# A four-layer GRU stack with an FFN behind it on one core: scan factors from PSUM to SBUF, two gate banks in place of three, five ring banks in place of four

## The chip, the cores and the metric

The kernel runs on one core of a Trainium2 chip. The metric is the device time in microseconds (us) of one execution. The core has a tensor engine (PE, its weight loads are shown as PEld), a vector engine (DVE), a scalar engine (ACT), GpSimd (POOL) and SyncE (SP), which only issues DMAs here. Each runs its own instruction list in order. They meet through semaphores alone. The on-chip memory is SBUF, and PSUM with eight banks of 128 x 512 fp32, into which PE writes.

## The reference

```python
x = x + xcond(layernorm(x), ctx, cond, fusion_W, fusion_b, gamma, beta)
x = x + ffn(layernorm(x), W_fc, ln_w, ln_b, W_proj)

# xcond, forward and backward in time with the same weights, 4 layers:
z = sigmoid(h @ Wz + bz);  h_tilde = tanh(h @ Wz + bz)     # one product serves both
a = clip(1 - z, 1e-8, 1 - 1e-8)
h_t = a_t * h_{t-1} + z_t * h_tilde_t                        # scan over 512 tokens
h = layernorm(h_new + h) * gamma + beta                      # the + h from layer 1 on
# then concat(forward, backward) @ fusion_W.T + fusion_b

# ffn: gelu(x @ sign_quantised(W_fc).T), layernorm over 2048, @ sign_quantised(W_proj).T
```

Shapes: x is 8 x 512 x 512 (batch, tokens, features), all fp32. The stack has 4 layers of 512 x 512.

## The kernel before

**Stage 1, the GRU stack.** The work is cut in 56 jobs (batch, direction, layer). In layer 0 one job serves both directions. A job has four parts m of 128 features each. Part m of job k has the number i = 4k + m. Its way through the engines is:

- PE, `mm` (L499): 12 matmuls (high and low halves of operands and weights) into a gate bank.
- ACT, `gates` (L796, L797): sigmoid of the bank into `zb`, then tanh of the same bank into `hb`. Both have three buffers in SBUF.
- DVE, `keep` (L1067): the factor max(1 - zb, tiny), written over the gate bank in PSUM. `tiny` is a PSUM column.
- POOL, `value` (L1521): hb = zb * hb.
- DVE, `scan` (L1080, in layer 0 L1088 and L1089 for the two directions): a `tensor_tensor_scan` of the factor and `hb`, 512 long, into `zb` (layer 0: into `H`).
- POOL, `add` (L1530): H = H + zb, in layers 1 to 3.

What follows a job is its tail. PE transposes H to token order (`tokens`, L519) into a ring bank, DVE takes the statistics (`stats`, L1100 to L1108), POOL the inverse root (`inv`, L1540 to L1545), ACT normalises into a buffer `ntok` (`norm`, L808), PE transposes back (`back`, L533) into a ring bank, ACT writes H and the high half AH (`feature`, L833, L837) and DVE the low half AL (`low`, L1117). AH and AL feed the next layer's matmuls.

Every engine walks over the same slots s, one job for each, with an order of operations written out by hand. The lists `RING_SLOT`, `FEAT_SLOT`, `LOW_SLOT` repeat that order, so that the semaphores' targets can be counted. Beside the jobs run preparations of the second stage's weights. In slots 24 to 55 that is on POOL `excess` (L1596 and L1598).

Of PSUM, banks 0 to 2 are the gate banks, banks 3 to 6 the ring, and bank 7 holds small things. `mm` number i waits until scan i - 3 is done, since that scan reads the factor out of its bank. A user n of the ring waits in `claim` until the last reader of user n - 4 is done.

**Stage 2** is the fusion matmul, the second layernorm and the FFN. DVE sums the activations there with L1297 and makes low halves with L1283. POOL sums the squares with L1640. These two engines' instructions have all tensors in SBUF.

Of the kernel before, what the change touches and what calls it, by code (L numbers as in the profile page):

```python
# [85 lines left out]
def batch(s):  # L86
# [129 lines left out]
def pixart_block(nc, x, wt, cond, fwt, fb, gamma, beta, fct, lnw, lnb, pjt, out):  # L216
# [64 lines left out]
    ntok = [sb(p1, f"ntok{i}", [128, 4, 512]) for i in range(3)]  # L281
# [58 lines left out]
    GATE, RING = PS[0:3], PS[3:7]  # L340
    TURNED, HIDDEN, PROJ = PS[0], (PS[1], PS[7]), PS[3:7]

    FUSED = {(u, h): RING[BANK[("F", u, h)] % 4] if u < 4 else PS[2] for u in range(NU) for h in range(2)}
# [70 lines left out]
    def _(e):  # L414
        def claim(n):

            if n < 4:
                return
            u = USERS[n - 4]
# [17 lines left out]
        def shift(l):  # L437

            n = BANK[("W", l)]
            claim(n)  # L440
            p = slice(0, 1) if l in BY_ROW else slice(0, 128)
            if l in BY_ROW:
                e.wait_ge(s_rc, BY_ROW.index(l) + 1)
            else:
                e.wait_ge(s_fo, KC * FOLDED.index(l) + KC)
            for m in range(KC):
                r = e.matmul(RING[n % 4][:, m:m + 1], bw[l][p, m * 128:(m + 1) * 128], ones[p, :], start=True, stop=True)
            r.then_inc(s_bp, 1)

        def fold_row(l):  # L450
# [16 lines left out]
        def add_rows(h):
# [5 lines left out]
            for q in range(KC):  # L473
                r = e.matmul(RING[n % 4][0:2, :], gb[:, q, :], xbuf1[:, q, :], start=(q == 0), stop=(q == KC - 1))
            r.then_inc(s_gp, 1)

        def mm(k, m):
# [5 lines left out]
            if i >= 3:  # L483
                e.wait_ge(s_sc, i - 2)
            n = 0
            for q in range(KC):
# [11 lines left out]
                for w, a in ((WH[l], AH[s]), (WL[l], AH[s]), (WH[l], AL[s])):  # L498
                    r = e.matmul(GATE[i % 3][:], w[:, q, m * 128:(m + 1) * 128], a[:, q, :], start=(n == 0), stop=(n == 11))  # L499
# [3 lines left out]
        def tokens(tau, pr):  # L503
# [11 lines left out]
            for i in range(2):  # L515
                n, c = BANK[("T", tau, pr, i)], (2 * pr + i) * 128
                claim(n)
                for m in range(KC):
                    r = e.transpose(RING[n % 4][:, m * 128:(m + 1) * 128], H[s][:, m, c:c + 128], ident[:])  # L519
                r.then_inc(s_t1, 1)  # L520

        def back(what, idx, m):
# [3 lines left out]
            n, w = BANK[(what, idx, m)], NTOK[(what, idx)] % 3  # L526
# [5 lines left out]
            for i in range(4):  # L532
                r = e.transpose(RING[n % 4][:, i * 128:(i + 1) * 128], ntok[w][:, i, m * 128:(m + 1) * 128], ident[:])  # L533
# [35 lines left out]
        def fc(j):  # L569
# [5 lines left out]
            if j == 0:  # L575
                e.wait_ge(d_fc, 32)
# [131 lines left out]
        for s in SLOTS:  # L708
            if s == SUM_SLOT:
                add_up()  # L710
            if s in ROW_SLOT:
                add_rows(ROW_SLOT.index(s))
            mm(job(s), 0)
            back("x", batch(s + 1), 1)
            back("x", batch(s + 1), 0)
            back("h", tail_b(s - 3), 2)
            back("h", tail_b(s - 3), 1)
            mm(job(s), 1)
            back("h", tail_b(s - 3), 3)
# [9 lines left out]
            mm(job(s), 3)  # L729
            tokens(tail_b(s - 2), 1)  # L730
            tokens(tail_b(s - 1), 0)
# [40 lines left out]
    def _(e):  # L772
# [7 lines left out]
        def gates(k, m):  # L780
# [15 lines left out]
            e.activation(zb[c][:], GATE[c][:], ACT.Sigmoid, bias=bias[:, l, m:m + 1]).then_inc(s_z, 1)  # L796
            e.activation(hb[c][:], GATE[c][:], ACT.Tanh, bias=bias[:, l, m:m + 1]).then_inc(s_t, 1)  # L797

        def norm(tau, pr):
# [5 lines left out]
            if w >= 3 and NORMED[p] < NORMED[("h", tau, 1 - pr)]:  # L805
                e.wait_ge(s_t2, max(T2N[(*NTOK_OF[w - 3], m)] for m in range(KC)) + 1)
            for i in range(2):
                e.activation(ntok[w % 3][:, 2 * pr + i, :], RING[BANK[("T", tau, pr, i)] % 4][:], ACT.Identity,  # L808
                             bias=nbp[:, r, i:i + 1], scale=rsp[:, r, i:i + 1]).then_inc(s_nt, 1)

        def norm_x(b):
# [5 lines left out]
            if w >= 3:  # L817
                e.wait_ge(s_t2, max(T2N[(*NTOK_OF[w - 3], m)] for m in range(KC)) + 1)
            for i in range(4):
                if b == 0 and i % 2 == 0:  # L820
                    e.wait_ge(s_xb, i // 2 + 1)
                e.activation(ntok[w % 3][:, i, :], (xbuf1 if b == 1 else xbuf)[:, i, :], ACT.Identity, bias=nb[:, b % 2, i:i + 1],
                             scale=rs[:, b % 2, i:i + 1]).then_inc(s_xn, 1)

        def feature(what, idx, m):
# [4 lines left out]
            n, s = BANK[u] % 4, 2 * (idx % 2) if what == "x" else place(TAILS[idx])  # L830
# [23 lines left out]
        def take_row(l):  # L854

            e.wait_ge(s_fr, BY_ROW.index(l) + 1)
            e.activation(bw[l][0:1, :], RING[BANK[("V", l)] % 4][0:1, :], ACT.Copy).then_inc(s_rc, 1)

        def take_rows(h):
# [5 lines left out]
            e.activation(dst, RING[BANK[("G", h)] % 4][0:2, :], ACT.Copy).then_inc(s_gr, 1)  # L865
# [8 lines left out]
        def aside(s):  # L874
# [3 lines left out]
            if PREP0 + 8 < s <= PREP0 + NPREP:  # L878
                sign(s - PREP0 - 1)
            if ABS0 <= s < ABS0 + 16:  # L880
                absolute(2 * (s - ABS0))
                absolute(2 * (s - ABS0) + 1)
# [125 lines left out]
        for s in SLOTS:  # L1008
            feature("h", tail(s - 4), 0)
            feature("h", tail(s - 4), 1)  # L1010
            feature("h", tail_b(s - 5), 0)
            feature("h", tail(s - 4), 3)
            feature("x", batch(s - 1), 3)
# [46 lines left out]
    def _(e):  # L1060
        def keep(k, m):
# [5 lines left out]
            e.scalar_tensor_tensor(GATE[c][:], zb[c][:], 1.0, tinyp.broadcast_to([128, S]), ALU.subtract, ALU.max,  # L1067
                                   reverse0=True).then_inc(s_a, 1)

        def scan(k, m):  # L1070
# [17 lines left out]
            e.tensor_tensor_scan(H[s][:, m, :], GATE[c][:], hb[c][:], 0.0, ALU.mult, ALU.add).then_inc(s_sf, 1)  # L1088
            e.tensor_tensor_scan(H[s + 1][:, m, :][:, ::-1], GATE[c][:, ::-1], hb[c][:, ::-1], 0.0, ALU.mult,  # L1089
                                 ALU.add).then_inc(s_sc, 1)  # L1090

        def stats(tau, pr):
# [17 lines left out]
        def low(what, idx, m):  # L1110
# [6 lines left out]
            e.tensor_tensor(AL[s][:, m, :], RING[BANK[u] % 4][:], AH[s][:, m, :].bitcast(F32), ALU.subtract).then_inc(s_al, 1)  # L1117
# [62 lines left out]
        def biases(l):  # L1180

            e.wait_ge(s_bp, l)
            e.tensor_tensor(cnd[:, l, :], RING[BANK[("W", l)] % 4][:, 0:KC], condt[:, l, :], ALU.add).then_inc(s_cn, 1)

        def aside(s):
# [3 lines left out]
            if s == ABS0 + 16:  # L1189
                for w in range(2):  # L1190
                    e.wait_ge(s_abs, 32)
                    e.reduce_sum(ssum[:, w:w + 1], asum[:, 16 * w:16 * w + 16], axis=AX_X).then_inc(s_ss, 1)
# [786 lines left out]
```

## Time and profile before

| | |
|---|---|
| median of 3 runs | 1590.77 us (1590.26 to 1591.34) |
| span of the profiled execution | 1589.6 us |
| its own time beside the span | none is given; the median lies 1.2 us above the span |
| PE busy in the span | 1532.7 us, 96% |
| DVE | 1372.7 us, 86% |
| POOL | 1127.2 us, 71% |
| ACT | 1030.8 us, 65% |
| granted TensorE clock | 1.00 of full speed in all slices |

Busy time is the time in which an engine executes something. Waits on semaphores are not in it. A wait for anything inside an instruction is in it and makes that instruction longer.

### The profile page before, as it was taken

What the parts mean: (1) busy time and instruction counts of PE and PEld (TensorE: products, weight loads), DVE (VectorE), ACT (ScalarE), POOL (GpSimd) and SP (SyncE); (2) the same over time, 40 slices, a digit from 0 to 9 for tenths busy, and PEclk for the clock granted to TensorE, in tenths of its full rate; (3) what the DMA queues carried; (4) which work ended last, traced back from release to release, by engine and by line L of the source; (5) the groups of instructions that cost most, each with busy time, mean ns of one, the idle gap of its engine ahead of it and who ended that gap; (6) DMA issues with size and microseconds to landing.
All of it is one profiled execution on the core that took longest, in us unless ns stands there. A gap on an engine that the chain in (4) does not pass through costs nothing.

```text
span 1589.6 us, 22972 instructions
## 1 busy us (share of the span) xinstructions
PE 1532.7 (96%) x7690; PEld 1255.9 (79%) x7690; DVE 1372.7 (86%) x2155; ACT 1030.8 (65%) x1689; POOL 1127.2 (71%) x1028
## 2 busy tenths in 40 slices
PE   7999999989989999999999999999999999999999
PEld 5777877777878778878778878888888888888887
DVE  7987999988999989899988897888887878787877
ACT  6887878888677788677787734444444444445454
POOL 4876877778979779979779864665565656555666
PEclk9999999999999999999999999999999999999999
DMA  4111231412302010312214462020201111120101
GB/s 166 41 53 54 74 97 36 145 55 87 126 34 87 34 54 34 120 35 79 93 39 154 154 221 84 20 87 20 85 22 60 47 61 47 39 68 23 45 14 40
DMA packets 72866, 112.68 MB, mean 71 GB/s; under 512 B 5159, under 2 KB 37927, under 8 KB 69678
## 3 DMA queue, kind: packets, MB, share of 16 engines
q1 hardware_dynamic: 72750, 111.21, 20.7%
q8 instruction: 63, 1.03, 0.3%
q14 instruction: 53, 0.43, 0.1%
HBM read 73.43 MB, written 37.76 MB: 70 GB/s over the span
## 4 chain that ended last, share of the span: by engine, by line
PE 66%; POOL 12%; DVE 9%; ACT 8%; issue 4%; DMA 0%; SPq 0%; POOLq 0%; DVEq 0%; ACTq 0%
PE ps L499 17%; PE ps L585 15%; PE ps L604 14%; PE ps L553 11%; POOL hb L1521 4%; POOL H L1530 4%; PE ps L533 3%; PE ps L519 3%; DVE bnp L1100 2%; ACT ntok L808 2%; ACT hb L797 2%; DVE H L1088 2%; DVE H L1089 1%; POOL rsp L1542 1%; DVE AL L1117 1%
## 5 line engine op out<-in xcount | busy, mean ns | idle before, releaser
L499 PE MATMUL ps<-AH,WH 128*128 128x512 f32 x896 | 366.9, 410 | 6.8 <-DVE H L1089 5.0
L1521 POOL TENSOR_TENSOR hb<-zb,hb 128x512 f32<-128x512 f32 x224 | 289.3, 1292 | 111.4 <-ACT hb L797 110.8
L499 PE MATMUL ps<-AL,WH 128*128 128x512 f32 x896 | 350.8, 392 | 0.0
L499 PE MATMUL ps<-AH,WL 128*128 128x512 f32 x896 | 350.0, 391 | 0.0
L1640 POOL TENSOR_TENSOR acq<-acq,sq 128x512 f32<-128x512 f32 x120 | 181.8, 1515 | 152.0 <-ACT sq L926 151.3
L1080 DVE TENSOR_TENSOR_SCAN zb<-ps,hb 128x512 f32<-128x512 f32 x192 | 234.1, 1219 | 38.6 <-POOL hb L1521 35.4
L1530 POOL TENSOR_TENSOR H<-H,zb 128x512 f32<-128x512 f32 x192 | 249.1, 1298 | 7.5 <-DVE zb L1080 5.1
L913 ACT ACTIVATE g<-ps 128x512 f32<-128x512 f32 x128 | 76.5, 598 | 249.3 <-PE ps L585 249.3
L1283 DVE SCALAR_TENSOR_TENSOR gl<-g,wcol,gh 128x512 fp32r<-128x512 f32 x118 | 133.6, 1132 | 93.3 <-ACT gh L923 93.3
L796 ACT ACTIVATE zb<-ps,cnd 128x512 f32<-128x512 f32 x192 | 133.1, 693 | 121.2 <-PE ps L499 110.8
L499 PEld LDWEIGHTS ps<-AH,WH 128*128 128x128 f32 x896 | 168.7, 188 | 42.1 <-DVE H L1089 7.7
L499 PEld LDWEIGHTS ps<-AL,WH 128*128 128x128 f32 x896 | 168.3, 188 | 37.1
L499 PEld LDWEIGHTS ps<-AH,WL 128*128 128x128 f32 x896 | 169.1, 189 | 29.4
L1297 DVE TENSOR_TENSOR acc<-acc,g 128x512 f32<-128x512 f32 x120 | 189.3, 1577 | 0.0
L1117 DVE TENSOR_TENSOR AL<-ps,AH 128x512 fp32r<-128x512 f32 x224 | 148.8, 680 | 27.6 <-ACT AH L837 26.8
L1100 DVE BATCH_NORM_STATS2 bnp<-ps 128x6 f32<-128x512 f32 x256 | 163.6, 680 | 2.0 <-PE ps L519 1.9
L808 ACT ACTIVATE ntok<-ps,nbp,rsp 128x512 f32<-128x512 f32 x192 | 139.2, 780 | 35.7 <-POOL nbp L1545 35.4
L833 ACT ACTIVATE H<-ps,bet,gam 128x512 f32<-128x512 f32 x192 | 154.6, 805 | 10.4 <-PE ps L533 10.0
L1067 DVE SCALAR_TENSOR_TENSOR ps<-zb,ps 128x512 f32<-128x512 f32 x224 | 152.6, 681 | 8.2 <-ACT hb L797 7.8
L519 PE MATMUL ps<-ident,H 128*128 128x128 f32 x1024 | 135.1, 274 | 16.5 <-ACT ntok L808 11.5
L533 PE MATMUL ps<-ident,ntok 128*128 128x128 f32 x896 | 121.0, 278 | 27.8 <-ACT ntok L808 13.8
L533 PEld LDWEIGHTS ps<-ident,ntok 128*128 128x128 f32 x896 | 102.2, 142 | 55.6 <-ACT ntok L808 31.2
(172 smaller groups left out, 3356.2 us busy)
## 6 DMA issues: line engine op xcount, KB each, us to landing
hs_scratch<-H SPq DMA_DIRECT2D x16, 1024.0 KB, 5.5
hc<-hs_scratch SPq DMA_DIRECT2D x32, 512.0 KB, 4.4
xr<-in_x SPq DMA_DIRECT2D x32, 256.0 KB, 4.5
out<-ob SPq DMA_DIRECT2D x32, 256.0 KB, 2.2
xbuf<-in_x SPq DMA_DIRECT2D x7, 1024.0 KB, 8.6
RAW<-in_wt SPq DMA_DIRECT2D x16, 256.0 KB, 7.1
stg<-in_fct SPq DMA_DIRECT2D x16, 256.0 KB, 3.3
stg<-in_pjt SPq DMA_DIRECT2D x16, 256.0 KB, 2.7
```

Source lines behind the costliest of these rows:

```text
L499: r = e.matmul(GATE[i % 3][:], w[:, q, m * 128:(m + 1) * 128], a[:, q, :], start=(n == 0), stop=(n == 11))
L519: r = e.transpose(RING[n % 4][:, m * 128:(m + 1) * 128], H[s][:, m, c:c + 128], ident[:])
L533: r = e.transpose(RING[n % 4][:, i * 128:(i + 1) * 128], ntok[w][:, i, m * 128:(m + 1) * 128], ident[:])
L553: r = e.matmul(FUSED[u, h][:], a[u % 2][:, q, :], w[:, q, :], start=(n == 0), stop=(n == 11))
L585: r = e.matmul(HIDDEN[j % 2][:], FC[q][:, c * 128:(c + 1) * 128], a[b % 2][:, q, :], start=(n == 0), stop=(n == 7))
L604: r = e.matmul(PROJ[t][:], a[BUFFER[j]][:, t * 128:(t + 1) * 128], PJ[c], start=(c == 0 and a is gh), stop=(c == NC - 1 and a is gl))
L1080: e.tensor_tensor_scan(zb[c][:, rv], GATE[c][:, rv], hb[c][:, rv], 0.0, ALU.mult, ALU.add).then_inc(s_sc, 1)
L1100: e.bn_stats(bnp[:, r, i, :], RING[BANK[u] % 4][:]).then_inc(s_bs, 1)
L1297: e.tensor_tensor(acc[b % 2][:], acc[b % 2][:], g[j % 2][:], ALU.add).then_inc(f_s1, 1)
L1521: e.tensor_tensor(hb[c][:], zb[c][:], hb[c][:], ALU.mult).then_inc(s_p, 1)
L1530: e.tensor_tensor(H[s][:, m, :], H[s][:, m, :], zb[i % 3][:], ALU.add).then_inc(s_v, 1)
L1640: e.tensor_tensor(acq[b % 2][:], acq[b % 2][:], sq[:], ALU.add).then_inc(f_s2, 1)
```

## The change

- The factor goes to a new SBUF tile `ab` (three buffers), and the scans read both inputs from SBUF.
- With that the gate banks are free after the tanh. There are two of them (PS[0] and PS[2]), and `mm` number i waits for tanh i - 2.
- The ring has five banks, and a user n waits for user n - 5.
- `ntok` has two buffers where it had three, which makes room for `ab`. `norm` waits for the backs of the tail two before it.
- In the second stage `fc(0)` has one more wait (`f_x1` at 8), since its bank is in the ring now.
- The slot lists and the calls in the slot loops are written in another order. The reordered pairs never both exist in one slot, so each engine issues the same operations in the same order as before.

```diff
-    ntok = [sb(p1, f"ntok{i}", [128, 4, 512]) for i in range(3)]
+    ntok = [sb(p1, f"ntok{i}", [128, 4, 512]) for i in range(2)]
+    ab = [sb(p1, f"ab{i}", [128, S]) for i in range(3)]
+    sb(p1, "free", [128, 512])
...
-    GATE, RING = PS[0:3], PS[3:7]
+    GATE = (PS[0], PS[2])
+    RING = [PS[(1, 3, 4, 5, 6)[(i - BANK[("F", 3, 1)]) % 5]] for i in range(5)]
...
         def claim(n):
 
-            if n < 4:
-                return
-            u = USERS[n - 4]
+            if n < 5:
+                return
+            u = USERS[n - 5]
...
-            if i >= 3:
-                e.wait_ge(s_sc, i - 2)
+            if i >= 2:
+                e.wait_ge(s_t, i - 1)
...
-                    r = e.matmul(GATE[i % 3][:], w[:, q, m * 128:(m + 1) * 128], a[:, q, :], start=(n == 0), stop=(n == 11))
+                    r = e.matmul(GATE[i % 2][:], w[:, q, m * 128:(m + 1) * 128], a[:, q, :], start=(n == 0), stop=(n == 11))
...
             if j == 0:
+                e.wait_ge(f_x1, 8)
                 e.wait_ge(d_fc, 32)
...
-            if w >= 3 and NORMED[p] < NORMED[("h", tau, 1 - pr)]:
-                e.wait_ge(s_t2, max(T2N[(*NTOK_OF[w - 3], m)] for m in range(KC)) + 1)
+            if w >= 2 and NORMED[p] < NORMED[("h", tau, 1 - pr)]:
+                e.wait_ge(s_t2, max(T2N[(*NTOK_OF[w - 2], m)] for m in range(KC)) + 1)
...
-            e.scalar_tensor_tensor(GATE[c][:], zb[c][:], 1.0, tinyp.broadcast_to([128, S]), ALU.subtract, ALU.max,
+            e.scalar_tensor_tensor(ab[c][:], zb[c][:], 1.0, tinyp.broadcast_to([128, S]), ALU.subtract, ALU.max,
                                    reverse0=True).then_inc(s_a, 1)
...
-                e.tensor_tensor_scan(zb[c][:, rv], GATE[c][:, rv], hb[c][:, rv], 0.0, ALU.mult, ALU.add).then_inc(s_sc, 1)
+                e.tensor_tensor_scan(zb[c][:, rv], ab[c][:, rv], hb[c][:, rv], 0.0, ALU.mult, ALU.add).then_inc(s_sc, 1)
...
-            e.tensor_tensor_scan(H[s][:, m, :], GATE[c][:], hb[c][:], 0.0, ALU.mult, ALU.add).then_inc(s_sf, 1)
-            e.tensor_tensor_scan(H[s + 1][:, m, :][:, ::-1], GATE[c][:, ::-1], hb[c][:, ::-1], 0.0, ALU.mult,
+            e.tensor_tensor_scan(H[s][:, m, :], ab[c][:], hb[c][:], 0.0, ALU.mult, ALU.add).then_inc(s_sf, 1)
+            e.tensor_tensor_scan(H[s + 1][:, m, :][:, ::-1], ab[c][:, ::-1], hb[c][:, ::-1], 0.0, ALU.mult,
                                  ALU.add).then_inc(s_sc, 1)
```

## Rows read from the trace of the kernel before

**Rows 1.** Windows by stage: length, then busy time of each engine (instructions), clock, DMA share.

```profile
0.00:923.00 923.00, 869.54 (x4678) 712.18 (x4679) 828.12 (x1549) 727.05 (x1213) 739.94 (x754) 1.00 0.23 81
923.00:1589.00 666.00, 663.19 (x3013) 543.70 (x3012) 544.63 (x607) 303.74 (x477) 387.25 (x275) 1.00 0.18 57
```

**Rows 2.** Groups of PE's matmuls, 0 to 923: busy, mean ns, idle before them.

```profile
L499 PE MATMUL ps<-AH,WH 128*128 128x512 f32 x896 | 366.9, 410 | 6.8 <-DVE H L1089 5.0 <-DVE zb L1080 1.8
...
L519 PE MATMUL ps<-ident,H 128*128 128x128 f32 x1008 | 133.2, 274 | 16.5 <-ACT ntok L808 11.5 <-DVE AL L1117 5.0
L533 PE MATMUL ps<-ident,ntok 128*128 128x128 f32 x896 | 121.0, 278 | 27.8 <-ACT ntok L808 13.8 <-ACT ntok L822 10.9 <-DVE AL L1117 2.6
```

**Rows 3.** The chain of waits from 512 to 560: start, us, what.

```profile
512.98 1.31 POOL hb L1521
514.28 1.24 POOL H L1530
...
520.24 1.25 POOL hb L1521
...
529.80 1.11 DVE H L1089
```

**Rows 4.** Groups of DVE, 0 to 923.

```profile
L1080 DVE TENSOR_TENSOR_SCAN zb<-ps,hb 128x512 f32<-128x512 f32 x192 | 234.1, 1219 | 38.6 <-POOL hb L1521 35.4
...
L1067 DVE SCALAR_TENSOR_TENSOR ps<-zb,ps 128x512 f32<-128x512 f32 x224 | 152.6, 681 | 8.2 <-ACT hb L797 7.8
L1117 DVE TENSOR_TENSOR AL<-ps,AH 128x512 fp32r<-128x512 f32 x224 | 148.8, 680 | 27.6 <-ACT AH L837 26.8
L1088 DVE TENSOR_TENSOR_SCAN H<-ps,hb 128x512 f32<-128x512 f32 x32 | 39.0, 1219 | 8.9 <-POOL hb L1521 5.2 <-issue 3.2
```

**Rows 5.** Groups of POOL, 0 to 923.

```profile
L1521 POOL TENSOR_TENSOR hb<-zb,hb 128x512 f32<-128x512 f32 x224 | 289.3, 1292 | 111.4 <-ACT hb L797 110.8
L1530 POOL TENSOR_TENSOR H<-H,zb 128x512 f32<-128x512 f32 x191 | 247.9, 1298 | 7.5 <-DVE zb L1080 5.1 <-ACT H L833 2.3
...
L1598 POOL TENSOR_TENSOR stg<-raw,stg 128x512 f32<-128x512 f32 x32 | 41.3, 1292 | 2.7
```

**Rows 6.** Single lines: count, duration min/median/max in ns.

```profile
L1080 DVE TENSOR_TENSOR_SCAN zb<-ps,hb x192: 1205/1223/1226, 61.1 to 921.5; 128x512 f32<-128x512 f32 x192
...
L1297 DVE TENSOR_TENSOR acc<-acc,g x120: 676/1779/1794, 952.3 to 1576.4; 128x512 f32<-128x512 f32 x120
```

**Rows 7.** DVE's timeline in stage 2, two stretches: start, us, what.

```profile
952.30 0.68 DVE L1297 TENSOR_TENSOR acc<-acc,g 128x512 f32<-128x512 f32 x1
...
1003.42 1.77 DVE L1283 SCALAR_TENSOR_TENSOR gl<-g,wcol,gh 128x512 fp32r<-128x512 f32 x1
```

**Rows 8.** POOL's timeline from 1003.

```profile
1003.32 1.33 POOL L1640 TENSOR_TENSOR acq<-acq,sq 128x512 f32<-128x512 f32 x1 [0.37 <-ACT sq L926]
1004.61 1.73 POOL L1662 TENSOR_TENSOR x<-x,cB 128x512 f32<-128x512 f32 x1
```

**Rows 9.** DVE's timeline, 510 to 516 (stage 1).

```profile
511.19 1.22 DVE L1080 TENSOR_TENSOR_SCAN zb<-ps,hb 128x512 f32<-128x512 f32 x1 [0.18 <-POOL hb L1521]
...
512.91 1.28 DVE L1117 TENSOR_TENSOR AL<-ps,AH 128x512 fp32r<-128x512 f32 x2
514.39 1.22 DVE L1080 TENSOR_TENSOR_SCAN zb<-ps,hb 128x512 f32<-128x512 f32 x1 [0.20 <-POOL hb L1521]
```

**Rows 10.** POOL's timeline, the same stretch.

```profile
511.04 0.71 POOL L1540 TENSOR_TENSOR rl<-vep,nhalf 128x2 f32<-128x2 f32 x1
511.72 1.30 POOL L1530 TENSOR_TENSOR H<-H,zb 128x512 f32<-128x512 f32 x1
512.98 1.31 POOL L1521 TENSOR_TENSOR hb<-zb,hb 128x512 f32<-128x512 f32 x1
514.23 1.29 POOL L1530 TENSOR_TENSOR H<-H,zb 128x512 f32<-128x512 f32 x1
515.57 1.29 POOL L1521 TENSOR_TENSOR hb<-zb,hb 128x512 f32<-128x512 f32 x1
```

More of the change, by code:

```diff
@@ L339, in pixart_block @@
     PS = [ctx.enter_context(nc.psum_tensor(f"ps{i}", [128, 512], F32)) for i in range(8)]
-    GATE, RING = PS[0:3], PS[3:7]
+    GATE = (PS[0], PS[2])
+    RING = [PS[(1, 3, 4, 5, 6)[(i - BANK[("F", 3, 1)]) % 5]] for i in range(5)]
     TURNED, HIDDEN, PROJ = PS[0], (PS[1], PS[7]), PS[3:7]
-    FUSED = {(u, h): RING[BANK[("F", u, h)] % 4] if u < 4 else PS[2] for u in range(NU) for h in range(2)}
+    FUSED = {(u, h): RING[BANK[("F", u, h)] % 5] if u < 4 else PS[2] for u in range(NU) for h in range(2)}
     tinyp = PS[7][:, 0:1]
@@ L525, in back @@
                 return
-            n, w = BANK[(what, idx, m)], NTOK[(what, idx)] % 3
+            n, w = BANK[(what, idx, m)], NTOK[(what, idx)] % 2
             if what == "h":
@@ L729, in _ @@
             mm(job(s), 3)
+            tokens(tail_b(s - 1), 0)
             tokens(tail_b(s - 2), 1)
-            tokens(tail_b(s - 1), 0)
             tokens(tail(s - 1), 1)
@@ L816, in norm_x @@
                 e.wait_ge(s_xb, b + 2)
-            if w >= 3:
-                e.wait_ge(s_t2, max(T2N[(*NTOK_OF[w - 3], m)] for m in range(KC)) + 1)
+            if w >= 2:
+                e.wait_ge(s_t2, max(T2N[(*NTOK_OF[w - 2], m)] for m in range(KC)) + 1)
             for i in range(4):
@@ L821, in norm_x @@
                     e.wait_ge(s_xb, i // 2 + 1)
-                e.activation(ntok[w % 3][:, i, :], (xbuf1 if b == 1 else xbuf)[:, i, :], ACT.Identity, bias=nb[:, b % 2, i:i + 1],
+                e.activation(ntok[w % 2][:, i, :], (xbuf1 if b == 1 else xbuf)[:, i, :], ACT.Identity, bias=nb[:, b % 2, i:i + 1],
                              scale=rs[:, b % 2, i:i + 1]).then_inc(s_xn, 1)
@@ L829, in feature @@
             u = (what, idx, m)
-            n, s = BANK[u] % 4, 2 * (idx % 2) if what == "x" else place(TAILS[idx])
+            n, s = BANK[u] % 5, 2 * (idx % 2) if what == "x" else place(TAILS[idx])
             e.wait_ge(s_t2, T2N[u] + 1)
@@ L856, in take_row @@
             e.wait_ge(s_fr, BY_ROW.index(l) + 1)
-            e.activation(bw[l][0:1, :], RING[BANK[("V", l)] % 4][0:1, :], ACT.Copy).then_inc(s_rc, 1)
+            e.activation(bw[l][0:1, :], RING[BANK[("V", l)] % 5][0:1, :], ACT.Copy).then_inc(s_rc, 1)
         def take_rows(h):
@@ L864, in take_rows @@
             dst = (raw0[0:2, :], xbuf1[0:2, 0, :])[h]
-            e.activation(dst, RING[BANK[("G", h)] % 4][0:2, :], ACT.Copy).then_inc(s_gr, 1)
+            e.activation(dst, RING[BANK[("G", h)] % 5][0:2, :], ACT.Copy).then_inc(s_gr, 1)
         def sign(n):
@@ L1182, in biases, with centred, sums_abs @@
             e.wait_ge(s_bp, l)
-            e.tensor_tensor(cnd[:, l, :], RING[BANK[("W", l)] % 4][:, 0:KC], condt[:, l, :], ALU.add).then_inc(s_cn, 1)
-        def aside(s):
+            e.tensor_tensor(cnd[:, l, :], RING[BANK[("W", l)] % 5][:, 0:KC], condt[:, l, :], ALU.add).then_inc(s_cn, 1)
+        def centred(s):
             if PREP0 <= s < PREP0 + 8:
                 center(s - PREP0)
[L1189 to L1192, printed above, removed]
+        def sums_abs():
+            for w in range(2):
+                e.wait_ge(s_abs, 32)
+                e.reduce_sum(ssum[:, w:w + 1], asum[:, 16 * w:16 * w + 16], axis=AX_X).then_inc(s_ss, 1)
         def bias_rows(h):
@@ L1200, in bias_rows @@
                 e.wait_ge(s_gv, 1)
[L1201 removed]
+            e.tensor_tensor(fbb[0:2, :], RING[BANK[("G", h)] % 5][0:2, :], fbb[0:2, :], ALU.add).then_inc(s_gv, 1)
         def center(n):
```

77 lines of the change are left out of this document (41 added, 36 removed).

## The prediction

> **What bounds the kernel now.** I read the windows first, cut at the end of the stack [rows 1]. In stage 2 (923 to 1589 us) PE is busy 663 of 666 us, and the change adds only one wait there (below). So everything is decided in stage 1: 923 us, PE busy 869.5, DVE 828.1, POOL 739.9, ACT 727.1. PE is idle 53 us, DVE 95, POOL 183. The reader is to see that two engines are near their limit at once. Next come PE's groups, for what ended its idle time [rows 2]: of its waits 6.8 us are for scans, which hold a gate bank, 5.0 + 2.6 for L1117 and 11.5 for L808, which hold a ring bank. The other 13.8 and 10.9 us of L533 I count as waits for data. That is 25.9 us which more banks could give back. Last the chain of waits inside stage 1 [rows 3]: it runs over POOL's products and adds, piece behind piece, and then over DVE's scans. DVE and POOL set the pace in such slots, and PE has waits because they are late. A cost on these two is a cost in time.
>
> **The change, part by part.** *The order of operations* is what it was: the pairs that change places (an x and a tail's transposes) never both exist in a slot. 0 us.
>
> *Keep writes SBUF.* L1067 has one SBUF tensor and a PSUM column in, and now SBUF out. The nearest row is L1117, one PSUM and one SBUF tensor in, SBUF out: 680 ns against 681 [rows 4]. I take 0; the bound is their difference, 224 x 1 ns, on either side.
>
> *Two gate banks.* Mm i waits for tanh i - 2 where it waited for scan i - 3. Between the two lie a POOL product and a scan on the other side of the tanh, so the wait gets shorter: at most 6.8 us back [rows 2], at least 0. *Five ring banks*: at most 11.5 + 5.0 + 2.6 = 19.1 us back, at least 0. I take 0 for both in the sum, since a PE that starts earlier still hands its result to DVE and POOL, which are slower after the change (next part).
>
> *Two ntok buffers.* Norm's new wait is for the backs of the tail two before. On PE those backs stand ahead of the tokens whose normalisation waits, so the tokens themselves come later than what is waited for. 0; if it did wait, the gates behind it on ACT would be late, and with them keep and value. *fc(0)'s wait for x1*: feat(3) stands ahead of it on PE and needs the same x1. 0.
>
> *The scans read two SBUF tensors.* This is the part that costs. First what the trace shows of DVE and POOL side by side. The scan, whose factor is in PSUM, takes 1205 to 1226 ns in all 192 cases [rows 6], though POOL is busy in 80% of the stage [rows 1]: it is never disturbed. L1297 has both inputs in SBUF. Alone it takes 0.68 us [rows 7]; over its 120 cases it is 676 at least and 1779 in the median [rows 6]. How it comes to that shows at 1003 us [rows 7, 8]. L1283 starts at 1003.42, while POOL's L1640 runs from 1003.32 to 1004.65. It ends at 1005.19, that is 0.54 after POOL's end, where it would need 0.68 alone: it stood still until 0.14 before POOL's end. And POOL's next one, L1662, started at 1004.61, ends at 1006.34, 1.15 after L1283's end: it stood still too, until 0.14 before DVE's end, and then took its 1.29. So one waits for the other whole instruction, and they take turns. After the change each scan has this form, and POOL's products and adds have it already.
>
> The Trainium skill (SBUF — State Buffer, "Who interferes with whom") says the same and speaks against this change: a vector instruction with two SBUF inputs contends with a GpSimd instruction that reads SBUF, and the second one to start blocks until the first is through. No run here shows a scan with two SBUF inputs; by that rule the sum below stands, without it the first rival does.
>
> What it costs in a slot I step through at 511 us [rows 9, 10]. Before: scan 511.19 to 512.41; add 511.72 to 513.02; product 512.98 to 514.28; then the next scan, which waited for it, 514.39 to 515.61; the add behind it had started at 514.23, 0.05 before the product's end; product 515.57 to 516.86. After: the first scan starts beside the small 128x2 POOL operation (511.04), which I take as no hindrance. The add stands until 512.41 - 0.14 = 512.27 and ends at 513.56. The product, 1.31 long and starting 0.04 before that end as it did before, ends at 514.83. The scan is ready at 514.93, but the add started at 514.78, ends at 516.07, and holds it until 515.93: the scan ends at 517.15, 1.54 late. The next product waits for that and ends at 518.30, 1.44 late. Two scans cost 1.5 us on both engines, 0.75 each.
>
> The bounds of this price. Below: timing independent of each other. POOL's 128x512 operations with SBUF inputs are 289.3 + 247.9 + 41.3 us [rows 5], with L1596 and small groups about 636 (an estimate), 69% of 923. A scan that starts beside one waits half of 1.29 less 0.14, 0.5 us: 0.69 x 0.5 = 0.34 us a scan. Above: each scan waits for a whole one, 1.29 - 0.14 = 1.15. The two scans of a layer-0 part come back to back, with a product queued between [rows 3, 4], and pay near that. There are 192 + 32 + 32 = 256 scans (L1089 has as many as L1088). I take 0.7, by the stepped slot, the nearest row: 256 x 0.7 = 179 us on DVE; bounds 87 and 294.
>
> Not all of that becomes time. DVE's 95 us of idle are partly waits for PE and ACT (26.8 for L837, 7.8 for L797 [rows 4]), and these shrink when DVE is what is late. I let 54 us be absorbed, some 60% of the idle, which leaves DVE 828 + 179 = 1007 busy in 1048 us. POOL has as much room: 740 + about 150 of standing still.
>
> **Sum.** 1589.6 (span) + 0 (order, keep, ntok, fc) - 0 (banks) + 179 - 54 = 1714.6, and 1.2 between this execution's span and the median of the runs: 1716 us, 8% slower.
>
> **The rivals.** *The lock bites, but the idle time swallows most of it.* For it: 95 and 183 us of idle. Against it: the chain lies on POOL and DVE themselves. At 0.34 us a scan, 87 us, with half absorbed: +44, 1635; the case reaches from 1596 to 1640.
>
> *The scan isn't hindered* (other side). It needs 1.22 us for 512 elements where L1117 needs 0.68 [rows 4], so it reads at half the pace and might share with POOL. Nothing else speaks for it. Then the banks are all that is left: 25.9 us at most, half of it passed on: -13, 1578, from 1565 to 1589. It decides if a scan's added time stays under some 0.1 us: 256 x 0.1 = 26.
>
> *POOL becomes the bound outright.* In the slots with L1596 and L1598 its work is densest, the chain lies on it [rows 3], and every product waits for a scan before it can release the next. At 1.0 us a scan and no more than 54 absorbed: 256 - 54 = +202, 1793; from 1765 up.
>
> *Nothing moves*: the scan isn't hindered and PE's waits only change their name: 1591.
>
> **How the numbers follow.** Within 0.2% (3.2 us) a measurement can't tell the kernels apart. Forecast (1640 to 1765): 0.70. Absorbed: 0.12. POOL bound: 0.07. Unhindered scan: 0.08. Nothing: 0.03. Range: leaving out the fastest 0.11 and the slowest 0.07 gives 1615 to 1770. Slower 0.89, same 0.03, faster 0.08.
>
> **What would show it.** L1080's group: a mean well over 1219 ns, 1.7 to 2.1 us, minimum near 1.2, maximum near 2.4. L1521 and L1530 over 1292 ns, with maxima near 2.3. L1067's group unchanged at about 681. DVE's busy time in stage 1 near 1000 us, the stage near 1048 long, stage 2 still about 666. PE's waits for scans at its gate banks gone from the list, but its idle time larger, for L808 and L1117. I am wrong if the scans' mean stays at 1.22, or if it is 1.9 and the stage is hardly longer.

## The result, and the profile after

| | before | changed |
|---|---|---|
| median of 4 runs | 1590.97 us | 1713.28 us (1711.91 to 1714.78) |
| ratio | | 1.077, 95% interval 1.0757 to 1.0783 |
| span of the profiled execution | 1589.6 us | 1710.0 us |

The change makes the kernel 122 us slower; 1716 was forecast. The windows of the changed kernel, cut where its last scan ends, answer to [rows 1]:

```profile
0.00:1043.00 1043.00, 900.52 (x4684) 739.67 (x4685) 911.73 (x1549) 726.92 (x1213) 896.01 (x754) 0.97 0.21 72
1043.00:1710.00 667.00, 662.32 (x3008) 542.52 (x3006) 545.44 (x607) 303.10 (x476) 387.51 (x275) 1.00 0.17 57
```

Stage 1 is 120 us longer (1043 against 923), stage 2 is what it was. In stage 1 DVE is busy 84 us more, POOL 156 us more, ACT as long as before. The granted clock is 0.97: 19 times in the stage it fell to the lower of its two levels (1.2 and 2.4 GHz). PE is busy 31 us more. DVE's idle time, 95 us before, is now 131.

The groups of DVE and of POOL in stage 1 answer to [rows 4] and [rows 5]:

```profile
L1088 DVE TENSOR_TENSOR_SCAN zb<-ab,hb 128x512 f32<-128x512 f32 x192 | 301.1, 1568 | 71.3 <-POOL hb L1533 69.8
...
L1075 DVE SCALAR_TENSOR_TENSOR ab<-zb,ps 128x512 f32<-128x512 f32 x224 | 150.0, 670 | 6.6 <-ACT hb L801 6.3
L1125 DVE TENSOR_TENSOR AL<-ps,AH 128x512 fp32r<-128x512 f32 x224 | 145.9, 675 | 30.2 <-ACT AH L841 30.2
L1097 DVE TENSOR_TENSOR_SCAN H<-ab,hb 128x512 f32<-128x512 f32 x32 | 49.6, 1550 | 0.0
L1096 DVE TENSOR_TENSOR_SCAN H<-ab,hb 128x512 f32<-128x512 f32 x32 | 47.6, 1489 | 13.3 <-issue 7.8 <-POOL hb L1533 5.1
```
```profile
L1533 POOL TENSOR_TENSOR hb<-zb,hb 128x512 f32<-128x512 f32 x224 | 355.8, 1589 | 79.1 <-ACT hb L801 78.9
L1542 POOL TENSOR_TENSOR H<-H,zb 128x512 f32<-128x512 f32 x191 | 260.2, 1362 | 8.7 <-DVE zb L1088 8.7
...
L1557 POOL TENSOR_TENSOR nbp<-nmp,rsp 128x2 f32<-128x2 f32 x96 | 55.4, 577 | 14.1 <-POOL rsp L1554 0.4
L1608 POOL TENSOR_SCALAR stg<-raw,th,nth 128x512 f32<-128x512 f32 x32 | 51.7, 1614 | 0.0
L1610 POOL TENSOR_TENSOR stg<-raw,stg 128x512 f32<-128x512 f32 x32 | 41.1, 1286 | 2.7
```

Two groups of POOL before, for comparison with L1608 and L1557:

```profile
L1596 POOL TENSOR_SCALAR stg<-raw,th,nth 128x512 f32<-128x512 f32 x32 | 24.8, 775 | 0.0
...
L1545 POOL TENSOR_TENSOR nbp<-nmp,rsp 128x2 f32<-128x2 f32 x96 | 20.2, 210 | 14.1 <-POOL rsp L1542 0.4
```

The reader is to see three things. First, the scans grew from 1219 to 1568 ns in the mean, and keep, next to them and on the same new tile, did not grow (670 against 681). Second, on POOL those instructions grew that start while a scan runs. Of the products 84 of 224 do, and take 2.09 us in the mean; the other 140 take 1.29. Of L1608 (L1596 before) 30 of 32 do, and its mean went from 775 to 1614 ns. L1610, right behind it, never does, and kept its length (1286 ns against 1292). Third, DVE's wait for the product rose from 35.4 to 69.8 us.

How an instruction gets longer shows in the timelines of DVE and POOL from 540 us. They are the same kind of stretch as [rows 9, 10]:

```profile
540.33 2.03 DVE L1088 TENSOR_TENSOR_SCAN zb<-ab,hb 128x512 f32<-128x512 f32 x1
542.28 0.66 DVE L1075 SCALAR_TENSOR_TENSOR ab<-zb,ps 128x512 f32<-128x512 f32 x1
542.97 1.84 DVE L1088 TENSOR_TENSOR_SCAN zb<-ab,hb 128x512 f32<-128x512 f32 x1
```
```profile
540.01 1.26 POOL L1533 TENSOR_TENSOR hb<-zb,hb 128x512 f32<-128x512 f32 x1 [0.48 <-ACT hb L801]
542.44 1.29 POOL L1542 TENSOR_TENSOR H<-H,zb 128x512 f32<-128x512 f32 x1 [1.16 <-DVE zb L1088]
543.69 2.21 POOL L1533 TENSOR_TENSOR hb<-zb,hb 128x512 f32<-128x512 f32 x1
```

The product runs to 541.27, and the scan that started at 540.33 ends at 542.36, 1.09 later. The add runs to 543.73, and the next scan ends at 544.81, 1.08 later. The product of 543.69 starts inside that scan and ends at 545.90, 1.09 after it. The forecast of an undisturbed length less 0.14 us holds for the scan to 0.01 (1.22 - 0.14 = 1.08). For the product it would be 1.15, and it is 0.06 less.

These are no picked cases. 115 of the 256 scans take over 1.24 us, and 110 of these end 1.06 to 1.11 us after the POOL instruction beside which they started. Of the products and adds that start inside a scan, 109 take over 1.4 us, and all of them end 1.05 to 1.10 us after that scan. The 22 scans that start while POOL runs nothing are all undisturbed. This is the turn-taking that [rows 7, 8] showed for other instructions of stage 2. The rule of the Trainium skill (SBUF — State Buffer, "Who interferes with whom") that the second one to start stands still agrees, and the trace now shows it for the scan too.

PE's groups answer to [rows 2]:

```profile
L502 PE MATMUL ps<-AH,WH 128*128 128x512 f32 x896 | 375.7, 419 | 3.0 <-ACT hb L801 1.5 <-DVE AL L1125 1.4
...
L536 PE MATMUL ps<-ident,ntok 128*128 128x128 f32 x896 | 134.0, 298 | 111.4 <-ACT ntok L812 95.5 <-ACT ntok L826 11.1 <-DVE AL L1125 4.9
L522 PE MATMUL ps<-ident,H 128*128 128x128 f32 x1008 | 133.6, 275 | 27.1 <-POOL H L1542 11.4 <-ACT ntok L812 8.1 <-DVE AL L1125 6.4
```

The waits for scans at the gate banks are gone, as meant. In their place stands the wait for ACT's normalisation, 95.5 us where it was 13.8. Read by itself this row accuses `ntok`, which lost a buffer. The list of all waits leads one step further: that normalisation waited for POOL (35.4 us before, 120.7 now), and the list has no wait of it for a buffer. The row before, then the row after (us in total, times, longest):

```profile
ACT ntok L808 <- POOL nbp L1545: 35.4, 38, 2.2
```
```profile
ACT ntok L812 <- POOL nbp L1557: 120.7, 73, 3.9
```

### The profile page after: what moved, and what is told of

Its sections match the earlier page's. It is cut to its first block, busy times and chain, and to the rows that moved or that the text cites. A ratio compares the mean times of both kernels' runs of the same rounds, so it can differ in the third digit from the quotient of the medians.

```text
span 1710.0 us, 22973 instructions
## 1 busy us (share of the span) xinstructions
PE 1562.8 (91%) x7690; PEld 1282.2 (75%) x7690; DVE 1457.2 (85%) x2155; ACT 1030.0 (60%) x1689; POOL 1283.5 (75%) x1028
## 4 chain that ended last, share of the span: by engine, by line
PE 44%; POOL 29%; DVE 13%; issue 8%; ACT 5%; DMA 0%; POOLq 0%; SPq 0%; DVEq 0%; ACTq 0%
PE ps L589 14%; PE ps L608 13%; POOL hb L1533 10%; PE ps L556 10%; POOL H L1542 8%; PE ps L502 3%; POOL rsp L1554 3%; DVE zb L1088 3%; DVE bnp L1108 2%; POOL nbp L1557 2%; PE ps L536 2%; DVE AL L1125 2%; POOL stg L1608 2%; DVE H L1096 2%; POOL stg L1610 1%
## 5 line engine op out<-in xcount | busy, mean ns | idle before, releaser
L1533 POOL TENSOR_TENSOR hb<-zb,hb 128x512 f32<-128x512 f32 x224 | 355.8, 1589 | 79.1 <-ACT hb L801 78.9
L502 PE MATMUL ps<-AH,WH 128*128 128x512 f32 x896 | 375.7, 419 | 3.0 <-ACT hb L801 1.5
L1088 DVE TENSOR_TENSOR_SCAN zb<-ab,hb 128x512 f32<-128x512 f32 x192 | 301.1, 1568 | 71.3 <-POOL hb L1533 69.8
L502 PE MATMUL ps<-AH,WL 128*128 128x512 f32 x896 | 357.3, 399 | 0.0
L502 PE MATMUL ps<-AL,WH 128*128 128x512 f32 x896 | 356.4, 398 | 0.0
L1542 POOL TENSOR_TENSOR H<-H,zb 128x512 f32<-128x512 f32 x192 | 261.4, 1362 | 8.7 <-DVE zb L1088 8.7
L536 PE MATMUL ps<-ident,ntok 128*128 128x128 f32 x896 | 134.0, 298 | 111.4 <-ACT ntok L812 95.5
L536 PEld LDWEIGHTS ps<-ident,ntok 128*128 128x128 f32 x896 | 113.1, 152 | 139.1 <-ACT ntok L812 112.2
L812 ACT ACTIVATE ntok<-ps,nbp,rsp 128x512 f32<-128x512 f32 x192 | 139.1, 777 | 120.8 <-POOL nbp L1557 120.7
L502 PEld LDWEIGHTS ps<-AH,WH 128*128 128x128 f32 x896 | 174.7, 195 | 36.7 <-ACT hb L801 2.6
L1075 DVE SCALAR_TENSOR_TENSOR ab<-zb,ps 128x512 f32<-128x512 f32 x224 | 150.0, 670 | 6.6 <-ACT hb L801 6.3
```

The lines of the kernel that those rows point to most:

```text
L502: r = e.matmul(GATE[i % 2][:], w[:, q, m * 128:(m + 1) * 128], a[:, q, :], start=(n == 0), stop=(n == 11))
L536: r = e.transpose(RING[n % 5][:, i * 128:(i + 1) * 128], ntok[w][:, i, m * 128:(m + 1) * 128], ident[:])
L1088: e.tensor_tensor_scan(zb[c][:, rv], ab[c][:, rv], hb[c][:, rv], 0.0, ALU.mult, ALU.add).then_inc(s_sc, 1)
L1533: e.tensor_tensor(hb[c][:], zb[c][:], hb[c][:], ALU.mult).then_inc(s_p, 1)
L1542: e.tensor_tensor(H[s][:, m, :], H[s][:, m, :], zb[i % 3][:], ALU.add).then_inc(s_v, 1)
```

## The experiments

Kernels of one group ran on the same chip beside the kernel before (1590.9 to 1592.0 us there). Where two experiments of different groups are compared, each one's ratio is.

### Parts of the change alone, and the suspected cost taken away

**The factors alone in SBUF.** The kernel before with `ab`, and two `ntok` buffers for the room.

```diff
-    ntok = [... for i in range(3)]
+    ntok = [... for i in range(2)]
+    ab = [sb(p1, f"ab{i}", [128, S]) for i in range(3)]
...
-            e.scalar_tensor_tensor(GATE[c][:], zb[c][:], 1.0, ...
+            e.scalar_tensor_tensor(ab[c][:], zb[c][:], 1.0, ...
...
-                e.tensor_tensor_scan(zb[c][:, rv], GATE[c][:, rv], hb[c][:, rv], ...
+                e.tensor_tensor_scan(zb[c][:, rv], ab[c][:, rv], hb[c][:, rv], ...
```

> The kernel before with the factors in SBUF (and two ntok buffers, which makes the room), but with its three gate banks, released by the scan, and its four ring banks. Theory (a scan with two SBUF inputs and a POOL operation that reads SBUF exclude each other): all of the loss comes with this edit alone, 1705 to 1725 us, the scans' mean duration 1.5 to 1.6 us with a maximum near 2.25, POOL's products near 1.6 us. Rival (the shorter list of gate banks or the new waits do it): at most 1.5% above the kernel before, 1615 us. If the new banks give something back inside the change, this kernel is slower than the changed one by up to 25 us.

Measured: 1717.17 us, ratio 1.0787 (1.077 to 1.0803). The interval overlaps with that of the whole change, so the 4 us between the two medians are not shown to be a difference. The scans' mean is 1570 ns, the products' 1593. All of the loss comes with this edit (it has the two `ntok` buffers too, which the next run tests); the rival's 1615 is out.

**Two ntok buffers alone.**

```diff
-            if w >= 3 and NORMED[p] < NORMED[("h", tau, 1 - pr)]:
-                e.wait_ge(s_t2, max(T2N[(*NTOK_OF[w - 3], m)] for m in range(KC)) + 1)
+            if w >= 2 and NORMED[p] < NORMED[("h", tau, 1 - pr)]:
+                e.wait_ge(s_t2, max(T2N[(*NTOK_OF[w - 2], m)] for m in range(KC)) + 1)
```

> The kernel before with two ntok buffers in place of three and nothing else. Theory: the wait for the tail two before is always over, 1590 to 1592 us, no difference. Rival (the longer idle time of PE for the normalisation, 112 us of waits on ACT's ntok in the changed kernel, comes from the missing third buffer): 1600 us or more.

Measured: 1591.11 us, ratio 0.9999 (0.999 to 1.0008). In the kernel before the third buffer is not needed. In the changed one the normalisation is idle for POOL alone, as shown above. So PE's 95.5 us of waits for it are the trail of POOL's lateness and not of the buffer.

**The changed kernel, scans with one SBUF input.** Every bank, buffer and wait of the change stays. Each scan, the two of layer 0 included, reads a PSUM column in place of `hb` and so leaves out the GRU's second operand.

```diff
-                e.tensor_tensor_scan(zb[c][:, rv], ab[c][:, rv], hb[c][:, rv], 0.0, ALU.mult, ALU.add).then_inc(s_sc, 1)
+                e.tensor_tensor_scan(zb[c][:, rv], ab[c][:, rv], tinyp.broadcast_to([128, S]), 0.0, ALU.mult, ALU.add).then_inc(s_sc, 1)
```

> The changed kernel whole, with its banks, buffers and waits, but each scan reads a PSUM column spread over 512 as its second input in place of hb, so it has one SBUF input; the scan's result is then not the GRU's. Theory: scans back to 1.22 us each and none longer, POOL's products back to 1.29, 1575 to 1591 us: the loss is gone and what the banks give shows alone (at most 25.9 us). Rival (waits of the change, a bank less for the gates, or the clock of PE): still above 1650 us.

Measured: 1591.32 us, ratio 1.0001 (0.9992 to 1.001). Its groups of scans and of POOL's products:

```profile
L1088 DVE TENSOR_TENSOR_SCAN zb<-ab,ps 128x512 f32<-128x512 f32 x192 | 233.5, 1216 | 39.7 <-POOL hb L1533 36.7
```
```profile
L1533 POOL TENSOR_TENSOR hb<-zb,hb 128x512 f32<-128x512 f32 x224 | 288.9, 1290 | 111.7 <-ACT hb L801 111.4
```

With a PSUM column in place of the second SBUF input scans and products have their old lengths, and the 122 us are gone. The loss needs the second SBUF input; all the rest of the change together comes to 0.4 us, within the noise. The last group returns to the banks.

**A PSUM bank for the factors, two gate banks.** An attempt at the gain without the price.

```diff
-    GATE, RING = PS[0:3], PS[3:7]
+    GATE, FACT, RING = (PS[0], PS[2]), PS[1], PS[3:7]
...
-            if i >= 3:
-                e.wait_ge(s_sc, i - 2)
+            if i >= 2:
+                e.wait_ge(s_t, i - 1)
...
+            if i > 0:
+                e.wait_ge(s_sc, i)
-            e.scalar_tensor_tensor(GATE[c][:], zb[c][:], 1.0, ...
+            e.scalar_tensor_tensor(FACT[:], zb[c][:], 1.0, ...
```

> The kernel before with one PSUM bank for the factors and two gate banks released by the tanh: keep i waits for scan i - 1, which stands ahead of it on DVE in any case. Scans keep one SBUF input. Ring and ntok as before. Theory: the waits of PE's gate matmuls for scans (6.8 us) go, and 0 to 7 us come back, 1584 to 1591 us. Rival (a gate bank less costs something since tanh now holds PE): 1595 us or more.

Measured: 1600.04 us, ratio 1.0056 (1.0043 to 1.0068). I expected a small gain and got a loss of 9.1 us, in the range of the rival, though PE's waits for scans are gone from its trace too. Below it is taken apart as far as it was tested.

### How much of it, and through which engine

**Half of the scans.**

```diff
+            f = GATE[c] if m < 2 else ab[c]
-            e.scalar_tensor_tensor(GATE[c][:], zb[c][:], 1.0, ...
+            e.scalar_tensor_tensor(f[:], zb[c][:], 1.0, ...
...
-                e.tensor_tensor_scan(zb[c][:, rv], GATE[c][:, rv], hb[c][:, rv], ...
+                e.tensor_tensor_scan(zb[c][:, rv], f[:, rv], hb[c][:, rv], ...
```

> As the kernel with the factors alone in SBUF, but the parts 0 and 1 of each job keep their factor in the gate bank, so half of the 256 scans have two SBUF inputs. Theory: half of those scans can be hindered, and half of the loss of that kernel shows: 1640 to 1670 us, and no scan that reads a factor from PSUM is over 1.24 us. Rival (the loss is a threshold, an engine that tips over into being the bound): all of it, 1700 us or more, or nearly nothing, under 1605 us.

Measured: 1644.51 us, ratio 1.0344 (1.0328 to 1.036), 53 us, 0.42 us for each of the 128 scans. It is neither all nor nearly nothing, so there is no threshold of the kind that the rival had. Where the loss sits surprised me. The scans from SBUF and from PSUM in layers 1 to 3 of this kernel:

```profile
L1084 DVE TENSOR_TENSOR_SCAN zb<-ab,hb 128x512 f32<-128x512 f32 x96 | 121.3, 1264 | 18.3 <-POOL hb L1525 17.0
L1084 DVE TENSOR_TENSOR_SCAN zb<-ps,hb 128x512 f32<-128x512 f32 x96 | 117.1, 1220 | 49.6 <-POOL hb L1525 48.7
```

The 96 scans from SBUF are hardly longer (1264 ns). That has to do with the half that was chosen, parts 2 and 3. Most of their scans start beside one of POOL's 128x2 operations: 105 of 128 in this kernel and in the changed one. In the changed kernel 100 of its 115 long scans are of parts 0 and 1, and 15 of parts 2 and 3. So this run is not half of the changed kernel's disturbed scans, and the 0.42 is no price that holds for either half. But the 96 scans from PSUM, none of them over 1.226 us, wait 48.7 us for POOL's products. DVE is idle 49.6 us before them, where before the same scans it was 29.4. DVE's busy time in its stage 1 is 838.3 us, 10 us more than before, and POOL's 810.9, 71 more. A stretch of it shows how that goes:

```profile
567.47 1.22 DVE L1092 TENSOR_TENSOR_SCAN H<-ab,hb 128x512 f32<-128x512 f32 x1
568.61 1.20 DVE L1093 TENSOR_TENSOR_SCAN H<-ab,hb 128x512 f32<-128x512 f32 x1
```
```profile
567.70 0.98 POOL L1549 TENSOR_TENSOR nbp<-nmp,rsp 128x2 f32<-128x2 f32 x1
568.64 2.25 POOL L1525 TENSOR_TENSOR hb<-zb,hb 128x512 f32<-128x512 f32 x1
```

No scan is longer than 1.22. POOL's small operation of 0.20 us starts inside the first scan and takes 0.98, and the product behind it starts inside both and takes 2.25, to 1.08 after the end of the second. DVE goes first and POOL pays, and POOL's next product is what later scans wait for.

**Layer 0 alone.** `f = ab[c] if JOBS[k][2] == 0 else GATE[c]`, otherwise as the one above.

> The same with the factor in SBUF in layer-0 jobs alone: 64 scans, 32 pairs back to back on DVE, where POOL's product of the next part is queued between the two. Theory, by the price of a scan in the changed kernel (122 us over 256 scans, 0.48 us each): 64 x 0.48 = 31 us, 1622 us, 1610 to 1640. If back-to-back pairs pay 1.05 us a scan, as the prediction's upper step has it: 1658 us.

Measured: 1624.96 us, ratio 1.0212 (1.0198 to 1.0226), 34 us, 0.53 us for each of 64 scans. The prediction had such pairs pay near its upper bound, 1.15 us (the expectation above says 1.05), and they cost less than half of that.

**A busier PE.** The changed kernel with one matmul of each gate product issued twice.

```diff
+                if q == 0:
+                    e.matmul(GATE[i % 2][:], WH[l][:, q, m * 128:(m + 1) * 128], AH[s][:, q, :], start=True, stop=True)
                 for w, a in ((WH[l], AH[s]), (WL[l], AH[s]), (WH[l], AL[s])):
```

> The changed kernel with the first matmul of each gate product issued twice, 224 matmuls of 0.2 us more (45 us of PE), the result unchanged. It asks whether the short falls of the granted clock in stage 1 (3.4 us at half speed each, 20 and more of them) are part of the loss. Theory (they are not, PE is not what is late): the falls get fewer, and the time stays within 5 us of the changed kernel, 1708 to 1720. Rival (the clock costs some 30 us, the rise of PE's busy time): 1690 or less if the falls go away.

Measured: 1717.85 us, ratio 1.0798 (1.0783 to 1.0813), against 1.077 for the change. The granted clock over the whole kernel is 0.988 where it was 0.980. The falls were fewer, not gone, and the time did not get shorter; PE is busy 38 us more in stage 1 (938.4 us against 900.5), and the kernel takes some 5 us more. So PE has room there. There are 12 falls in the stage where there were 19. Since they didn't all go away, this shows for a part of them only that the lower clock costs nothing that one can see.

**Less work on POOL.** Two of its preparation operations cut to two columns, in the kernel before and in the changed one:

```diff
-            e.tensor_scalar(stg2[n % 2][:], raw[n % 2][:], th[:, w:w + 1], ...
+            e.tensor_scalar(stg2[n % 2][:, 0:2], raw[n % 2][:, 0:2], th[:, w:w + 1], ...
...
-            e.tensor_tensor(stg2[n % 2][:], raw[n % 2][:], stg2[n % 2][:], ALU.subtract)...
+            e.tensor_tensor(stg2[n % 2][:, 0:2], raw[n % 2][:, 0:2], stg2[n % 2][:, 0:2], ALU.subtract)...
```

> The kernel before with POOL's two preparation operations of slots 24 to 55 cut from 512 columns to 2, so that the second stage's weights are not the right ones. It takes some 60 us of work off POOL. All theories: a little faster than before or the same, 1575 to 1591 us, since POOL stands in the chain of these slots.

> The changed kernel with the same cut. Against the other one with the cut it shows the loss when POOL has less to do. Theory (scans and POOL take turns, POOL's queue hands the delay on): the loss falls from 122 us to 90 to 110, since 64 of about 500 POOL operations that exclude a scan are gone. Rival (POOL is the bound outright in those slots): the loss falls by half or more, to 60 us or less. Rival (POOL's work doesn't matter, DVE alone carries it): it stays at 122.

Measured: 1585.99 and 1700.82 us, 115 us apart, where the full ones are 122 apart. With 47 us less on POOL in the kernel before (693.0 against 739.9 busy) and the densest slots relieved, the loss is 7 us smaller, and by the two intervals it may be 3 to 11. That misses the theory's 90 to 110 and is nearer to the 122 of the rival by which POOL's work doesn't matter, so it doesn't decide between these two; POOL as outright bound of those slots (60 or less) is out. The cut took away little that excludes a scan: of its two operations in the changed kernel only L1608 starts inside scans.

The windows of stage 1, each cut at its last scan, in the order layer 0, half, factors alone, changed with light POOL:

```profile
0.00:954.00 954.00, 877.55 (x4675) 715.71 (x4676) 849.89 (x1548) 726.56 (x1212) 781.15 (x754) 0.99 0.22 78
```
```profile
0.00:975.00 975.00, 882.39 (x4683) 720.83 (x4684) 838.30 (x1549) 727.17 (x1213) 810.94 (x754) 0.99 0.22 77
```
```profile
0.00:1053.00 1053.00, 917.94 (x4685) 735.02 (x4686) 913.98 (x1549) 727.37 (x1213) 898.03 (x754) 0.97 0.21 71
```
```profile
0.00:1032.00 1032.00, 896.03 (x4683) 736.78 (x4684) 910.78 (x1548) 727.80 (x1213) 855.67 (x754) 0.97 0.21 73
```

Against their own kernel before (stage 1 of 923 us, POOL 740; with light POOL 918 and 693), the stage grew by 31, 52, 130 and 114 us, POOL's busy time by 41, 71, 158 and 163, DVE's by 22, 10, 86 and 81. The growth of the stage is 0.7 to 0.8 of POOL's in all four. To DVE's it stands as 1.4, 5, 1.5 and 1.4. So the loss goes more nearly with the time that POOL stands still than with the time added on DVE. This is a correlation, and a loose one: with light POOL that time is the largest (163 us), and the loss is not. What shows the path itself is the wait for products in the kernel with half of the scans.

### What the banks are worth

**Keep waits for the scan before it.** The kernel before and one wait.

```diff
             e.wait_ge(s_t, i + 1)
+            if i > 0:
+                e.wait_ge(s_sc, i)
             e.scalar_tensor_tensor(GATE[c][:], zb[c][:], 1.0, ...
```

> The kernel before, three gate banks and all, with one wait more: keep i waits on the semaphore of scan i - 1, which stands ahead of it on the same engine. It asks why the kernel with a bank for the factors was 9 us slower. If that wait is it (DVE can't start keep in the scan's last 0.08 us): 1596 to 1602 us. If the missing third gate bank was it: 1590 to 1592 us.

Measured: 1594.22 us, ratio 1.0018 (1.0009 to 1.0026). The wait costs 2.9 us, less than the 5 and more that one of the two guesses gave it and more than the other's nothing. DVE's trace has only 0.5 us of waits for the scan. From the start of a scan to the start of the keep right behind it the kernel before has 1.14 us: the scan of 511.19 in [rows 9] takes 1.22, and keep starts 0.08 before its end.

```profile
512.33 0.67 DVE L1067 SCALAR_TENSOR_TENSOR ps<-zb,ps 128x512 f32<-128x512 f32 x1
```

The kernel with the wait:

```profile
512.41 1.22 DVE L1082 TENSOR_TENSOR_SCAN zb<-ps,hb 128x512 f32<-128x512 f32 x1
513.74 0.70 DVE L1069 SCALAR_TENSOR_TENSOR ps<-zb,ps 128x512 f32<-128x512 f32 x1
```

That is 1.33 us, 0.19 more, for an order that DVE's own list keeps anyway. In 104 of the 224 cases keep stands right behind a scan, and there the median goes from 1.141 to 1.327 us.

**Two gate banks and a ring of four**, and **three gate banks and a ring of four**, both with scans of one SBUF input. The first is the changed kernel with:

```diff
-    RING = [PS[(1, 3, 4, 5, 6)[(i - BANK[("F", 3, 1)]) % 5]] for i in range(5)]
+    RING = PS[3:7]
...
-            u = USERS[n - 5]
+            u = USERS[n - 4]
```

The second is the kernel with the factors alone in SBUF, with the scans changed as above.

> The changed kernel with scans of one SBUF input (a PSUM column in place of hb, so the result isn't the GRU's), two gate banks, and a ring of four banks in place of five. With five the time was that of the kernel before. If a gate bank less costs and a ring bank more gives that back: 1595 to 1600 us. If neither bank matters: 1590 to 1592 us.

> The kernel with the factors alone in SBUF and the banks of before (three gates, four in the ring), with the same scans of one SBUF input. Against the kernel with the factors alone in SBUF it takes away only the second SBUF input. Theory: 1590 to 1592 us, all of the 126 us gone. Rival (something of the move to SBUF beside the two inputs costs, such as keep's write): 1600 us or more.

Measured, with the changed kernel's variant from above as the third:

| gate banks, ring banks | median, us | ratio (interval) |
|---|---|---|
| 3, 4 (as before) | 1591.20 | 1.0000 (0.9991 to 1.0009) |
| 2, 4 | 1594.84 | 1.0023 (1.0014 to 1.0032) |
| 2, 5 (as changed) | 1591.32 | 1.0001 (0.9992 to 1.001) |

Two gate banks released by the tanh, in place of three released by the scan, cost 3.7 us, and the fifth ring bank gives 3.5 back. (The first of these steps has the change's wait of `fc(0)` and its order of calls in it, which were not tested alone.) In the one with 2 and 4 PE waits no more for scans, but 20.7 us for the normalisation (13.6 in the one with 3 and 4) and 6.2 for AL (5.0): the wait moved on along PE's list. The first row is also the sharpest test of the cause: it differs from the kernel with the factors alone, 1717 us, only in the second input of the scans. If the costs add up, the factor bank's 9.1 us are 2.9 for keep's wait and 3.7 for the gate bank; the last 2.5 stay open.

No kernel tried that does all of the work is faster than the one before.

## Why the prediction was right

**The bound.** That DVE and POOL set the pace of stage 1 held: a cost on them was a cost in time, and neither the banks nor 38 us more of PE's work changed it much.

**The mechanism** was right, to 0.01 us in single cases, from rows of other instructions in another stage [rows 7, 8]. That no row showed a scan of this form was the largest doubt. The scan takes 1.22 us where L1117 takes 0.68, and it holds POOL off for nearly all of that: the product of 543.69 ends 1.09 us after the scan and needs 1.29 alone.

**The price and what was absorbed** were both mis-sized, and that the sum came out 3 us from the measurement is luck. The step put 0.7 us a scan on DVE, 179 us, and let 54 of them vanish in DVE's idle time: 125 net. Measured, DVE's busy time rose by 84 us, 0.33 a scan, and its idle time did not shrink but grew by 36, from 95 to 131: 120 net.

The first error is in how the step was booked. Its second scan was to be 1.54 us late. Of that 1.00 is inside the scan (ready at 514.93, held until 515.93), which is busy time. The other 0.54 is a later start, because the product came later, and that is idle time of DVE. The step so gives 0.50 and 0.27 us a scan, 128 us busy and 69 idle over 256, and not 179 busy. The prediction booked the whole as busy time, and its "about 150 of standing still" on POOL (measured: 156) was not carried on to DVE's waits.

The second error is that the slot is dearer than the mean. In it one scan of two is held, for 1.00 us. Measured, 115 of 256 are over 1.24 us, and by 0.75 us in the mean: 0.34 a scan. By the timeline 108 of the 256 start beside one of POOL's 128x2 operations (L1552, L1554, L1557), and 106 of these are undisturbed, as the prediction took it. The idle time grew by 36 us where the step gives 69, and most of that is scans waiting for products, 69.8 us where it was 35.4. The lower bound's 0.34 was met by other factors than its own (0.69 of the scans held for 0.5 us each). The kernel with half of the scans shows how far the second path can go: its stage 1 is 52 us longer, with 10 more of DVE's busy time.

**Keep, order, ntok, fc** at 0: right as a sum, since the changed kernel with one-input scans takes 1591.32 us. Ntok was tested alone, order and fc were not. Keep got 11 ns shorter where a bound of 1 ns had been given; 224 of them are 2.5 us, and the kernel with three gate banks and one-input scans shows no change in the time.

**The banks** at 0: right in the sum of the two (1591.32), though not for the reason given. They don't bring nothing because DVE and POOL are slower after the change; with scans at full speed they bring nothing either. Fewer gate banks cost 3.7 us, where the prediction had said that they give at least 0, and the fifth ring bank gives 3.5.

**The rivals.** Absorbed (1596 to 1640), unhindered (1578), POOL as the bound (from 1765) and nothing (1591) are out. The first rested on 95 and 183 us of idle time. Of DVE's 95 us before, 40.6 were its scans' waits for POOL [rows 4], and this time did not take up POOL's delay but grew with it. (The prediction says that without the turn-taking the first rival would stand. It would be the second, the scan that isn't hindered.)

**The signs.** L1067's successor unchanged, PE's waits for scans gone, its idle time larger, stage 2 as before, stage 1 at 1043 for 1048: as said. The scans' mean was given as 1.7 to 2.1 us and is 1.57. Their maximum is 2.25 (near 2.4 was given), that of the products 2.27 and of the adds 2.21 (near 2.3 was given). DVE's busy time is 912, not near 1000.

## What to carry to other kernels

Before an operand of a busy DVE instruction moves from PSUM to SBUF, count its SBUF inputs. If it gets a second one while GpSimd works on SBUF data, expect what this case shows for the scan and for L1283 and L1297, that the two engines take turns. A row in the trace with an instruction of that form, disturbed and undisturbed, gives what one meeting costs. How many meetings there are depends on what stands beside each instruction, so step more than one slot, and book what is inside the instruction apart from what comes before it. Look for the loss on both engines and in the waits between them, since the one that comes first keeps its length and the other pays; the busy time of one engine alone can hide nearly all of it. Follow a wait that grew back to its root before a buffer is blamed, and test a bank's worth alone and without the other edits.

## What the runs showed of the hardware

- A `tensor_tensor_scan` with both inputs in SBUF takes turns with POOL's 128x512 operations, 1.22 us undisturbed and up to 2.25. With one input in PSUM it is never over 1.23, be it a bank (256 scans of the kernel before) or a spread column (256 of the changed kernel with one SBUF input).
- The turns overlap a little: 110 of 115 held scans end 1.06 to 1.11 us after POOL's instruction (1.22 alone), and 109 of 109 held products and adds 1.05 to 1.10 us after the scan (1.29 alone).
- What stands still on POOL is not only two-input work: the `tensor_scalar` L1608 with one 128x512 tensor in went from 775 to 1614 ns in the mean, and L1557, 128x2, from 210 to 577. What starts outside the scans, as L1610 does, keeps its length.
- The 128x2 operations of POOL hardly hold a scan in turn: 106 of 108 scans that start beside one kept their 1.22 us.
- A wait on the semaphore of the scan just ahead on DVE moves the next start by 0.19 us (median 1.141 to 1.327 in 104 pairs), and cost this kernel 2.9 us.
